# Moving the last three transposed loads and their small projections later in a 16-step loop (layernorm, recurrence and int8 FFN on eight cores)

## The reference

```python
xn = _layernorm(x)                       # x: (4, 4096, 2048)
# attention branch
xp = einsum('btd,ed->bte', xn, W_in)
dt = softplus(einsum('btd,hd->bth', xp, W_dt) + b_dt)     # 32 heads
a  = exp(dt[..., None] * -exp(log_A))
ys = associative_scan: y[t] = a[t] * y[t-1] + xp[t]        # along t
attn = einsum('btd,ed->bte', ys, W_out)
# FFN branch, int8 weights with a scale per output column
f   = silu((xn @ w_gate) * s_gate) * ((xn @ w_up) * s_up)  # 8192 wide
ffn = (f @ w_down) * s_down
out = x + attn + ffn
```

## Time and profile before

| | |
|---|---|
| median of 3 runs | 3556.18 us (3555.86 to 3560.6) |
| profiled execution: its time | 3558.29 us |
| profiled execution: span of its slowest core (core 3) | 3556.7 us |
| spans of the eight cores | 3539.2 to 3556.7 us |
| TensorE matmul busy | 3218.0 us, 90% of the span |
| ScalarE, VectorE busy | 528.3 us, 471.0 us |
| mean granted TensorE clock, core 3 | 0.969 |

### The profile page before, as it was taken

One profiled execution on the slowest core, in us unless ns is written; L12 is line 12 of the kernel. 1 busy time (PEld: TensorE's weight loads), 2 busy tenths in 40 slices (PEclk: granted clock), 3 DMA queues, 4 the chain that ended last, 5 costly groups with the idle time before them and its releaser, 6 DMA issues.

```text
span 3556.7 us, 36849 instructions; the slowest of 8 cores (3539.2 to 3556.7 us)
## 1 busy us (share of the span) xinstructions
PE 3218.0 (90%) x15088; PEld 1448.2 (41%) x15088; DVE 471.0 (13%) x537; ACT 528.3 (15%) x768; POOL 226.5 (6%) x318
## 2 busy tenths in 40 slices
PE   0156998999999999999999999969989997997999
PEld 0022443444444444444444444424434443443444
DVE  3252220000000000000000012200021004004000
ACT  2133342212221222122212221200000000000000
POOL 1000111000010001000010001000000000000000
PEclk9877999999999999999999999989989999999999
DMA  9674542211122111211122122366575557556653
GB/s 197 132 179 95 85 86 88 68 54 54 54 67 59 54 54 56 70 54 54 54 62 63 54 66 89 95 171 200 188 245 173 184 186 242 183 183 225 178 177 116
DMA packets 124677, 416.92 MB, mean 117 GB/s; under 512 B 49168, under 2 KB 49184, under 8 KB 109536
## 3 DMA queue, kind: packets, MB, share of 16 engines
q1 hardware_dynamic: 77264, 220.23, 19.7%
q0 software_dynamic: 44800, 176.52, 19.4%
q10 hardware_dynamic: 2448, 17.83, 1.7%
HBM read 321.33 MB, written 67.63 MB: 109 GB/s over the span
## 4 chain that ended last, share of the span: by engine, by line
PE 86%; DMA 7%; SPq 4%; DVE 2%; issue 1%; ACT 1%; POOL 0%; ACTq 0%; DVEq 0%; POOLq 0%
PE ps_g L617 25%; PE ps_u L617 25%; PE pso L734 24%; PE pso L728 6%; PE ps_xp L421 5%; SPq L314 3%; DMA wdq_sb<-wd 2%; DMA xtb<-x_full 1%; DMA xn_scr<-xnb 1%; DVE wdq_sb L552 1%; DMA ftb<-f_scr 1%; DMA xnT<-xn_scr 0%; DMA winNb<-winN 0%; PE psdtl L327 0%; DVE xsq_s L260 0%
## 5 line engine op out<-in xcount | busy, mean ns | idle before, releaser
L734 PE MATMUL pso<-wdq_sb,ftb 128*128 128x512 bf16 x4096 | 917.8, 385 | 62.5 <-DVE wdq_sb L552 62.5
L617 PE MATMUL ps_g<-xnT,wgb 128*128 128x512 bf16 x4032 | 880.5, 379 | 0.0
L617 PE MATMUL ps_u<-xnT,wub 128*128 128x512 bf16 x4032 | 880.5, 379 | 0.0
L734 PEld LDWEIGHTS pso<-wdq_sb,ftb 128*128 128x128 bf16 x4096 | 402.7, 99 | 566.8 <-issue 97.2
L617 PEld LDWEIGHTS ps_u<-xnT,wub 128*128 128x128 bf16 x4032 | 395.1, 98 | 475.1
L617 PEld LDWEIGHTS ps_g<-xnT,wgb 128*128 128x128 bf16 x4032 | 393.9, 98 | 476.3
L640 DVE TENSOR_TENSOR fb<-gb,ub 128x512 bf16<-128x512 bf16 x256 | 108.9, 425 | 1559.4 <-ACT ub L632 1559.4
L632 ACT ACTIVATE ub<-ps_u,su_c 128x512 bf16<-128x512 f32 x256 | 175.9, 687 | 709.3 <-PE ps_u L617 709.3
L629 ACT ACTIVATE gb<-ps_g,sg_c 128x512 bf16<-128x512 f32 x256 | 175.9, 687 | 703.1 <-PE ps_g L617 703.1
L728 PE MATMUL pso<-wo_sb,ytb 128*128 128x512 bf16 x1024 | 234.6, 383 | 28.8 <-DMA ftb<-f_scr 28.8
L421 PE MATMUL ps_xp<-xnT,winTb 128*128 128x512 bf16 (+1 forms) x1280 | 244.8, 351 | 0.0
(11 more groups left out here) (63 smaller groups left out, 548.8 us busy)
## 6 DMA issues: line engine op xcount, KB each, us to landing
ftb<-f_scr SPq DMA_DIRECT2D x64, 2048.0 KB, 11.0
ytb<-ys_scr SPq DMA_DIRECT2D x64, 512.0 KB, 11.6
f_scr<-fb POOLq DMA_DIRECT2D x64, 512.0 KB, 5.4
wdq_sb<-wd POOLq DMA_DIRECT2D x32, 1024.0 KB, 15.6
wgb<-wg POOLq DMA_DIRECT2D x63, 512.0 KB, 5.6
wub<-wu POOLq DMA_DIRECT2D x63, 512.0 KB, 6.3
xtb<-x_full ACTq DMA_DIRECT2D x17, 1024.0 KB, 11.6
winTb<-winT POOLq DMA_DIRECT2D x32, 512.0 KB, 7.0
```

The source lines that it names most:

```text
L617: inst = TE.matmul(ps[:, cols], wtile[:, dt * P:(dt + 1) * P], xnT[:, dt * T + WU + ch * 512: dt * T + WU + ch * 512 + 512], start=(dt == ...
L734: inst = TE.matmul(ps_o[ko][:, :], ft_b[kf][:, jt * P:(jt + 1) * P], wdq_sb[:, jt * QW:(jt + 1) * QW], start=False, stop=(jt == NJ - 1))
```

## The change

In pass 0's loop the five emissions of transposed loads and small projections for chunks 2, 3 and 4 sit after other steps. Before: loads of chunk 2 after step 4, its projection after 5, loads of 3 after 8, projection after 9, loads of 4 after 10, projection after 11. After the change: loads of 2 after step 11, projection after 12, loads and projection of 3 after 13, loads and projection of 4 after 14. The instructions themselves, their waits in the code and their number are the same, except that the spills which `wait_all` covers are those emitted by then. The layernorm's order (`fr`, `bk`) stays.

```diff
-            if et == 4:
+            if et == 11:
                 emit_tr(2)
-            elif et == 5:
+            elif et == 12:
                 emit_dtl(2)
-            elif et == 8:
+            elif et == 13:
                 emit_tr(3)
-            elif et == 9:
                 emit_dtl(3)
-            elif et == 10:
+            elif et == 14:
                 emit_tr(4)
-            elif et == 11:
                 emit_dtl(4)
```

## The result

The changed kernel's median is 3527.6 us in 8 runs, against 3559.8 in 10 runs of the kernel before on the same chip; the ratio is 0.9914, interval 0.9902 to 0.9927. Some executions on any chip are slow (the cores of a die show a lower granted clock); the ratios and all times named from here on leave them out, which the two medians do not. Forecast were 3521 with a range of 3505 to 3538: a gain of 35. Measured by the ratio it is 31 (0.86% of 3556). The slowest core of the profiled execution is now core 2, at 3526.4 us; core 2 of before ended at 3539.2, core 3 then at 3556.7.

The account below looks back on a forecast made before the run. TensorE's pass 0 waits on transposed loads were taken as the bound. First transpose 275.7, sets end 346.5, landing 352, projection 354.1, step 15 364.4; pass 1 there instead of 398.76 gains 34.4: 3556.2 - 34.4 = 3521.8, rounded to 3521; range 3505 to 3538.

Parts of the forecast that it names:

- The bound: Pass 0: TensorE waits on transposed loads, 74.5 us together for chunks 2 to 4; what pass 0 gives back reaches the end.
- the last projection: Pass 0, chunk 4's projection: 1.9 us, from 352.2 to 354.1, its dt work hidden by step 15.
- Layernorm's tail: Pass 0, from 229: tile 16 normalized by 267.1, its spill takes 8.3, chunk 2's loads start at 275.7.
- the second stall: Pass 0, before chunk 3's projection, 32.91 us: ScalarE stood behind the projection too, so tile 16's normalization ended only at 304.67.
- The sets: SyncE's queue: chunk 2's transposes 27 us, chunk 3's 22.3, chunk 4's 325.5 to 346.5; each weight-load burst costs 2.
- signs of being wrong: Sets over 27 us each, tile 16's spill out later than 280, or a new wait in step 15 or later.
- The landing and step 15: End of pass 0: chunk 4's loads land 5.5 us after issue, at 352; step 15 takes 10.3, to 364.4.
- everything behind pass 1 moves as a block: From pass 1 to the end: pass 1's earlier start, 364.4 instead of 398.76, carries through whole, gain 34.4.
- A: Transposes beside weight loads: chunk 0's 44.73 us for each of chunks 2 and 3, total 3563; chance 3 in 100.
- B: Transposes halted by weight loads: each burst costs its full 4.2 us, gain 19, total 3537; chance 15 in 100.
- C: TensorE's waits in pass 0 vanish: gain the whole 74.5 us, total 3482; chance 4.
- D: No change: the end is set outside pass 0, say by the last stage's DMA schedule, 3556; chance 2.

Follow-up runs that it names:

- e9: Changed kernel with chunks 3 and 4 loaded by one set of 640-row transposes, loads after steps 11 and 12, projections after 12, 14, 14; 3512.3 us, one time only.
- e2: Changed kernel without the winTb weight loads for steps 12 to 15 of pass 0 (wrong weights used); 3513 to 3518 us, ratio 0.9878.
- e6: Changed kernel with each winTb weight load for steps 12 to 15 made twice; 3534 to 3537 us, ratio 0.9941.
- e5: Changed kernel unaltered, run again for a second trace; 3520.8 to 3522.1 us, ratio 0.9902.
- e4: Changed kernel with spills of tiles 10 to 16 from ScalarE's queue, loads after steps 3, 7, 8, projections after 9, 13, 14; 3532 to 3556 us, ratio 0.9935.
- e7: e1 with only the spills of tiles 13 to 16 issued from ScalarE's queue; 3517 to 3562 us, ratio 0.9951.
- e11: e7 without the x loads for tiles 13 to 16 (computed from older rows, values wrong); 3509 and 3521 us, ratio 0.9870.
- e8: e1 one step earlier: loads after steps 3, 8, 9, projections after 11, 13, 14; 3517.4 and 3517.9 us, ratio 0.9891.
- e10: e1 with chunks 3 and 4 in one set of 640 rows, loads after steps 4 and 8, projections after 12, 13, 14; 3506.3 to 3514.8 us, ratio 0.9862.
- e1: Changed kernel with loads back at their earlier places (after steps 4, 8, 10), projections kept after 12, 13, 14; 3511 to 3514 us, ratio 0.9867.

## Why the prediction was right, and where it was lucky

**The bound.** That pass 1's start hangs on one chain (layernorm's tail, tile 16's spill, 48 transposes in SyncE's queue, the last projection, step 15) was right: shortening the queue's part moved pass 1 by most of it or as much (e9 by 13 to 17 for 20 us, with two cores that no longer wait for the last loads; e2 by 6 to 9 for 6), lengthening it too (e6: 8 to 11 for 10).

**Layernorm's tail.** Forecast 275.7 for the first transpose, measured 272.7 on core 2 (266.0 to 276.4 on the eight). The lowest of them is core 3's, the core that the forecast was made for: forecast 9.7 too late there, 5.7 of it because core 3 was already ahead when it began step 6 (222.4 in this execution, where before it was ready for it at 228.1). Counted from there the tail took 43.6 us on core 3 and 43.9 on core 2 (from 228.8), where I had 47.6 (228.1 to 275.7): about 4 too long. ScalarE's freedom from the second stall was the right reason: tile 16's spill starts at 264.4 on core 2, where core 3 of before had started it at 304.8.

**The sets.** 27, 22.3 and 21 forecast, 27.5, 21.7 and 20.9 measured on core 2. e2 and e6 show the cause of the first to be the weight loads, at 1.6 to 2.5 us each. Of the prediction's own signs of being wrong, one came in part: chunk 2's set took 24.7 to 28.6 us and was over 27 on three cores. No new wait came in a later stage, but the last stage's old ones grew in this trace.

**The landing and step 15.** I took 5.5 between 3.6 and 7.9. On four cores it was 2.4, below my lower bound; on the other four, where a weight load was in flight as well, 6.0 to 7.0 (core 3: load 336.2 to 342.9, last transpose 336.4 to 343.0). The sum also has a slip: the landings of the earlier trace rows count from the start of the last issue, and I added them behind the end of the sets, so about 1.2 us stands in it twice. The forecast for pass 1, 364.4, was 9.6 too late on core 2: 3.0 from layernorm, 0.7 from the sets, 4.4 from the landing with the slip in it, and 1.5 from the last projection (1.05 instead of 1.9) and step 15.

**The total.** The step "everything behind pass 1 moves as a block" is where the luck lies. The slowest core changed. From core 3 of before to core 2 of after, pass 1 starts 44.0 us earlier and the end comes 30.3 earlier: 11.3 went in the last stage (1198.1 to 1209.4), 1.4 in pass 1 and 1.0 in gate and up. My 34 lies near 31 since pass 1's start was mis-sized by 9.6 in one direction and the last stage by 11.3 in the other. On core 3 alone pass 1 starts 43.3 earlier and the end comes 35.5 earlier. On the means of all cores it is 33.2 at pass 1 and 26.3 at the end in this trace; over more executions the end's mean comes 28.8 earlier (seven of the changed kernel, the one trace of before), and 32.3 in e5 (three against nine). Whether the block moves as one on the mean of many executions these runs do not settle, since before was traced only once.

**The rivals.** A (chunk 0's price) did not come with the change, and with each weight load made twice (e6) chunk 2's set still took only 30.7 to 32.8 us; layernorm is done by then. It came where the loads ran beside layernorm with the spills in ScalarE's queue: chunk 2's set took over 44.7 us on five cores each of e4 and e7, and chunk 3's on three of e11, behind layernorm. With the spills in SyncE's queue it came on single cores (e8: 50.8 and 45.4, e10: 45.2). B (weight loads halt the transposes) would have cost 4.2 each; measured 1.6 to 2.5. By the rule of the Trainium skill (DMA: Bandwidth & Descriptors, Queues, rings and completion order), round the queues by packets, I had expected the small packets to get the smaller share; e2 and e6 agree that the sets lose by each weight load, not that they lose all of its 4.2. C needed chunk 2's loads to start at 239; e1 and e10 show how near one can come: the transposes' waits fall to 3.5 us and to nothing on the quick cores, but layernorm, whose spills then stand behind the set, takes 9.6 us of it. D fell with the result.

## What to carry to other kernels

Follow what stands in a queue behind and ahead of a moved transfer, and ask which engine a wait stops besides its own: here the projection's wait also stopped ScalarE's normalization, whose output the next loads needed, so one late load bred the next. A consumer's late place and a load's late place are two edits: moving the consumer late gave the gain, moving the loads late cost part of it. And with eight cores the slowest sets the time, so a schedule that is quicker on six and slow by chance on two, as e10, is worth less than its mean; e8, quick on three, was no gain on e1 at all.

## What the runs showed of the hardware that was not expected

Where little else is in flight, a DMA transpose occupies SyncE's queue for 1.2 to 1.3 us whether it moves 128 rows (chunk 4's in the changed kernel, 340.26: 1.23), 512 (320.35: 1.26) or 640 (e9: 1.27). Fewer and longer ones shorten the queue.

How long a transpose takes is not its own. The mean time of a packet in SyncE's queue was 20 ns for a set alone; over the 48 transposes it was 18 to 21 ns in e2, 21 to 25 in the changed kernel's first trace and 23 to 29 in e6, core by core. It was 74 on core 5 of e4, where core 4 of the same execution had 25, and 77 in one set of e11, with no x load and no spill of a normalized tile beside it. The last stage of the same kernel took core 2 1209.4 and 1199.8 us in two executions, with the same granted clock of 0.97 in it.
